# Layer norm of the next tile and the V projection moved into the heads of the K projection

## What is computed

```
xn = layernorm(x)
Q, K, V = xn@Wq+bq, xn@Wk+bk, xn@Wv+bv ; Q, K = rope(Q), rope(K)
s  = softmax(causal(Q K^T / 8)) V @ Wo + bo
g  = silu( layernorm(gelu(xn @ ternary(W_fc)^T)) @ ternary(W_proj)^T )
out = x + s * g
```

## Time and profile before

| what | value |
|---|---|
| median of 3 runs | 6779.58 us (6776.34 to 6803.11) |
| profiled execution, its own time | 6805.19 us |
| its span on the slowest core (core 1) | 6803.5 us |
| PE matmul busy, ACT busy, DVE busy | 48%, 37%, 11% of the span |
| mean granted TensorE clock, die 0 and die 1 | 0.785, 0.791 |
| K/V stage, 836 to 2890 us: busy PE, ACT, DVE | 732.9, 441.5, 266.8 us of 2054 |

### The profile page before, as it was taken

The page is one execution under the profiler, slowest core; times in us unless marked ns, Lnnn a source line. Parts: engine busy times, 40 slices in busy tenths (PEclk is TensorE's granted clock), DMA queues, the critical chain, the costliest instruction groups (busy, mean ns, idle before and its releaser), DMA issues.

```text
span 6803.5 us, 50659 instructions; the slowest of 8 cores (6769.1 to 6803.5 us)
## 1 busy us (share of the span) xinstructions
PE 3262.8 (48%) x13195; PEld 1049.8 (15%) x13195; DVE 766.9 (11%) x1887; ACT 2532.9 (37%) x4503; POOL 355.5 (5%) x598
## 2 busy tenths in 40 slices
PE   2333323432343234423566666666666433664666
PEld 0011111111111111111111111111111111121222
DVE  0122111111111111112100000000000121110000
ACT  2211222211221122223567778888888311111000
POOL 0122100000000000000111110100000000000000
PEclk9999966766677667766778888889998655787888
DMA  6311243345334533342111111111110111113222
GB/s 167 102 54 56 41 62 42 42 41 62 42 43 42 58 44 43 39 68 62 40 52 43 43 62 41 52 64 46 35 54 27 40 43 44 41 37 91 62 62 65
DMA packets 280346, 366.16 MB, mean 54 GB/s; under 512 B 149954, under 2 KB 231954, under 8 KB 272914
## 3 DMA queue, kind: packets, MB, share of 16 engines
q1 hardware_dynamic: 257922, 285.91, 22.0%
q10 hardware_dynamic: 4608, 43.26, 2.1%
q0 software_dynamic: 17552, 33.78, 2.0%
HBM read 299.50 MB, written 71.83 MB: 55 GB/s over the span
## 4 chain that ended last, share of the span: by engine, by line
PE 28%; ACT 28%; DMA 15%; issue 11%; DVE 8%; SPq 6%; POOL 2%; ACTq 1%; DVEq 0%; POOLq 0%
ACT Pbuf L689 11%; ACT Pbuf L692 8%; PE pb L414 5%; PE pb L838 5%; PE pb L485 4%; PE pb L940 4%; DMA xtile<-x_kv 3%; DMA wp_dram<-wps 3%; SPq L506 3%; SPq L524 2%; DMA hcol<-h_dram 2%; DMA wf<-Wfc 2%; ACT xnb L395 1%; DVE x2s L375 1%; PE pb L400 1%
## 5 line engine op out<-in xcount | busy, mean ns | idle before, releaser
L689 ACT ACTIVATE Pbuf<-pb,bias 128x512 bf16<-128x512 f32 x896 | 615.7, 687 | 232.6 <-PE pb L668 193.3
L400 PE MATMUL pb<-identb,xnb 128*128 128x128 bf16 x640 | 93.2, 265 | 1268.3 <-ACT xnb L395 1268.3
L710 PE MATMUL pb<-Pbuf,Vbuf 128*65 128x512 bf16 x1152 | 445.1, 386 | 389.7 <-ACT Pbuf L692 387.1
L692 ACT ACTIVATE Pbuf<-pb,bias 128x512 bf16<-128x512 f32 x896 | 609.8, 681 | 0.0
L668 PE MATMUL pb<-Q_sb,Kbuf 64*128 64x512 bf16 x1152 | 464.8, 403 | 0.0
L665 PE MATMUL pb<-Q_sb,Kbuf 64*128 64x512 bf16 x1152 | 464.6, 403 | 0.0
L713 PE MATMUL pb<-Pbuf,Vbuf 128*65 128x512 bf16 x1152 | 445.1, 386 | 0.0
L838 PE MATMUL pb<-xn5t,wfcT 128*128 128x512 bf16 x1024 | 328.5, 479 | 81.2 <-ACT wfcT L830 60.8
L940 PE MATMUL pb<-wpp,hcol 128*128 128x512 bf16 x1024 | 261.7, 420 | 211.1 <-DMA hcol<-h_dram 162.3
L372 ACT ACTIVATE x2s<-xtile 128x1024 bf16<-128x1024 f32 x80 | 84.7, 1058 | 721.0 <-DMA xtile<-x_kv 632.0
L485 PE MATMUL pb<-Wv_sb,xnT 128*128 128x512 bf16 (+1 forms) x1536 | 306.0, 361 | 76.2 <-ACT vraw L499 76.2
(11 more groups left out here) (170 smaller groups left out, 3990.3 us busy)
## 6 DMA issues: line engine op xcount, KB each, us to landing
xtile<-x_kv SPq DMA_DIRECT2D x64, 512.0 KB, 7.0
V_dram<-vraw SPq DMA_DIRECT2D x128, 132.0 KB, 21.1
Vbuf<-V_dram ACTq DMA_DIRECT2D x8, 2112.0 KB, 14.8
gtile<-Wfc SPq DMA_DIRECT2D x32, 512.0 KB, 3.4
gtile<-Wpj SPq DMA_DIRECT2D x32, 512.0 KB, 3.9
pj_f<-Wpj SPq DMA_DIRECT2D x8, 2048.0 KB, 8.0
t1s<-T1k SPq DMA_DIRECT2D x16, 1024.0 KB, 22.2
t2s<-T2k SPq DMA_DIRECT2D x16, 1024.0 KB, 22.9
```

Of the source, the lines that this page charges most:

```text
L400: pv = E("tensor", lambda e, fc=fc: e.transpose(tr_ps[:, fc * 128:(fc + 1) * 128], xnb[:, fc * 128:(fc + 1) * 128], identb[:]), waits=[("a ...
L689: e1 = E("scalar", lambda e, it=it, blo=blo: e.activation(out=Pbuf[it][:, 0:QTW], in_=sA[it][:, 0:QTW], func=AF.Exp, scale=0.125, bias=blo ...
L692: e2 = E("scalar", lambda e, it=it, bhi=bhi: e.activation(out=Pbuf[it][:, QTW:2 * QTW], in_=sB[it][:, 0:QTW], func=AF.Exp, scale=0.125, bi ...
L710: p1_ = E("tensor", lambda e, vsrc=vsrc, vcb=vcb, it=it, kc=kc, ntile=ntile: e.matmul(cA[0:65, 0:QTW], vsrc[:, vcb:vcb + 65], Pbuf[it][:, ...
```

## The change

The x loads, layer norm and transposes of tile 0 now stand ahead of the loop. For the others, `ln_and_transpose` is a generator that yields ahead of each of its four bodies, and `v_build` is split into `v_build_sub` (one sub of 128 rows) and `v_build_out` (the stores). A `filler` is called once a head within `rope_project`, between the projection of the next head and `keo` of this one: in odd heads it emits one sub of V of this tile, and in each head it advances the generator for the next tile by one step. The copy to `xnT` also waits for the PE work emitted before this tile. The tables are issued ahead of the heads of their tile, as before. The Q stage keeps its order.

```diff
-    def ln_and_transpose(x_src, tt, xnT_buf, marks, tw):
+    def ln_and_transpose(x_src, tt, xnT_buf, marks, tw, key):
         for sub in range(tw // 128):
+            yield
             i = sub % 2
...
-                in_=tr_ps[:].rearrange("p (f t) -> p f t", f=8)), waits=[("pe", pv)], inc="ac")
+                in_=tr_ps[:].rearrange("p (f t) -> p f t", f=8)),
+                waits=[("pe", pv), ("pe", marks.get(key + "_pefree", 0))], inc="ac")
             marks["tr_evac"] = av4
-        return av4
+            marks[key] = av4
...
         pmark = {0: emit_proj(0)}
+        filler = marks.pop("filler", None)
         for hp in range(HP):
             ei = hp % 2
             if hp + 1 < HP:
                 pmark[hp + 1] = emit_proj(hp + 1)
+            if filler is not None:
+                filler(hp)
...
-    def v_build(xnT_buf, tt, tw, marks):
+    def v_build_sub(xnT_buf, tt, tw, marks, subs):
         i = 0
         segs = [(0, 512), (512, 1024), (1024, VROW)]
-        for sub in range(tw // 128):
+        for sub in subs:
...
+    def v_build_out(tt, tw, marks):
+        i = 0
         av = M("ac")
...
+    gen = ln_and_transpose(x_kv, 0, xnT[0], marks, 512, "lnk0")
+    for _ in gen:
+        pass
     for tt in range(NT1):
         i = tt % 2
...
-        ln_and_transpose(x_kv, tt, xnT[i], marks, 512)
...
+        ni = (tt + 1) % 2
+        emit_tables(tt, T1k, T2k, 512)
         _rope_tab_gate[0] = marks["tab_q"]
-        rope_project(xnT[i][:], Wk_sb, bkc, t1s[i][:], t2s[i][:], ('K', tt), tt, 512, marks)
+        if tt + 1 < NT1:
+            marks[f"lnk{tt+1}_pefree"] = M("pe")
+            nxt = ln_and_transpose(x_kv, tt + 1, xnT[ni], marks, 512, f"lnk{tt+1}")
+        else:
+            nxt = iter(())
+
+        def filler(hp, tt=tt, nxt=nxt):
+            if hp % 2 == 1:
+                v_build_sub(xnT[tt % 2][:], tt, 512, marks, [(hp - 1) // 2])
+            next(nxt, None)
+
+        marks["filler"] = filler
+        rope_project(xnT[i][:], Wk_sb, bkc, t1s[0][:], t2s[0][:], ('K', tt), tt, 512, marks)
         marks["tab_reuse"] = M("dv")
-        v_build(xnT[i][:], tt, 512, marks)
...
+        for _ in nxt:
+            pass
+        v_build_out(tt, 512, marks)
```

More of the change, by code:

```diff
@@ L517, in build, with emit_tables @@
              "vps_reuse": M("ac"), "x2_reuse": M("dv"), "u_dv": M("dv")}
+    def emit_tables(tt, src1, src2, tw):
+        q1 = E("sync", lambda e, tt=tt, src1=src1, tw=tw: e.dma_start(
+            out=t1s[0][:].rearrange("p (h t) -> p h t", h=HP)[:, :, 0:tw],
+            in_=src1[:, :, tt * tw:(tt + 1) * tw].rearrange("h p t -> p h t")),
+            waits=[("dv", marks.get("tab_reuse", 0))], inc="q_t0", incval=16)
+        E("sync", lambda e, tt=tt, src2=src2, tw=tw: e.dma_start(
+            out=t2s[0][:].rearrange("p (h t) -> p h t", h=HP)[:, :, 0:tw],
+            in_=src2[:, :, tt * tw:(tt + 1) * tw].rearrange("h p t -> p h t")),
+            inc="q_t0", incval=16)
+        marks["tab_q"] = ("q_t0", M("q_t0"))
@@ L528, in build @@
-        marks["tab_q"] = ("q_t0", M("q_t0"))
-        ln_and_transpose(x_kv, tt, xnT[i], marks, 512)
-        marks.setdefault("xnT_hold", {})[i] = M("ac")
-        marks["tab_wait"] = marks["tab_q"]
-        _rope_tab_gate[0] = marks["tab_q"]
-        rope_project(xnT[i][:], Wk_sb, bkc, t1s[i][:], t2s[i][:], ('K', tt), tt, 512, marks)
+        ni = (tt + 1) % 2
+        emit_tables(tt, T1k, T2k, 512)
+        _rope_tab_gate[0] = marks["tab_q"]
+        if tt + 1 < NT1:
[3 more added lines that the diff above has]
+            nxt = iter(())
@@ L534, in build @@
+        def filler(hp, tt=tt, nxt=nxt):
[4 more added lines that the diff above has]
+        rope_project(xnT[i][:], Wk_sb, bkc, t1s[0][:], t2s[0][:], ('K', tt), tt, 512, marks)
         marks["tab_reuse"] = M("dv")
-        v_build(xnT[i][:], tt, 512, marks)
-        marks["tr_evac"] = max(marks.get("tr_evac", 0), 0)
-        marks[f"xnT_pe{i}"] = M("pe")
+        for _ in nxt:
+            pass
@@ L538, in build @@
+        v_build_out(tt, 512, marks)
     p1_done_q = M("qs")
     p1_done_pe = M("pe")
-    NQT = OWN // 512 if OWN >= 512 else 1
     QW = min(512, OWN)
@@ L544, in build @@
         i = tt % 2
[L545 to L553, removed]
+        emit_tables(tt, T1q, T2q, QW)
         _rope_tab_gate[0] = marks["tab_q"]
-        ln_and_transpose(x_own, tt, xnT[i], marks, QW)
+        marks[f"lnq{tt}_pefree"] = M("pe")
+        for _ in ln_and_transpose(x_own, tt, xnT[i], marks, QW, f"lnq{tt}"):
+            pass
         av = M("ac")
         for fc in range(8):
-            E("sync", lambda e, fc=fc, tt=tt, i=i: e.dma_start(
+            E("sync", lambda e, fc=fc, tt=tt, i=i, QW=QW: e.dma_start(
                 out=xn_dram[fc, :, tt * QW:(tt + 1) * QW],
                 in_=xnT[i][:, fc * QW:(fc + 1) * QW]), waits=[("ac", av)], inc="q_xn", incval=16)
-        rope_project(xnT[i][:], Wq_sb, bqc, t1s[i][:], t2s[i][:], ('Q', tt), tt, QW, marks)
+        rope_project(xnT[i][:], Wq_sb, bqc, t1s[0][:], t2s[0][:], ('Q', tt), tt, QW, marks)
         marks["tab_reuse"] = M("dv")
-        marks[f"xnT_q{i}"] = M("qs")
     p1b_done = M("ac")
```

## The result

| | before | after |
|---|---|---|
| median | 6801.43 us (10 runs) | 6872.6 us (9 runs) |
| ratio | | 1.0114, 95% interval 1.0086 to 1.0142 |
| same pair on a second chip | 6717.19 us | 6809.0 us, 1.0143, interval 1.0114 to 1.0172 |

The change makes the kernel slower, by 1.1 to 1.4%. The forecast was slower by 2.7%, with a range from 6820 to 7060 us. The sign held, and the norm was moved and not hidden, as forecast; the size was about twice too large, and most of that lies in one term, the wait for the tables. (Against 6779.58 us, the median at hand when it was made, the measured 6872.6 lies 93 us higher.)

What follows compares the result with a forecast made beforehand. No single engine owns the chain; a K/V tile is serial pieces, 136.9 us. With norm moved and table wait exposed, the period becomes 148.6; +182 us on the 6779.6 median gives 6961 us, range 6820 to 7060.

Steps and rivals of the forecast that it cites:

- The norm is moved, not hidden: K/V heads 1 to 4: norm bodies overlap neither V nor the same head's chain; 7.97 us each, four times a tile.
- Rival 1: K/V stage: ACT and DVE do the norm while PE does V and projections; -296 us, 6484 us; chance 0.07.
- The x loads: ACT waits 4.3 us for xtile in heads 2 and 4; projection and V hide the load in 1 and 3.
- The clock: PE in the K/V heads: after near idleness a projection takes 3.4 us, a sub of V the mean, 7.1.
- Rival 2: K/V stage: denser PE work keeps the clock high, so no change; about +1 us, 6781 us; chance 0.10 with nearby cases.
- The tables come about 39.8 us after V_dram: Head 0's first m1 waits for t1s and t2s, taken from the former x wait; 39.2 to 43.4 us.
- The sum: K/V stage: tile 0 +45.0, 14 periods of 148.6 against 136.9 us +163.8, last tile -26.8; together +182 us.
- Rival 3: K/V stage: tables later and V slow throughout; period over 154 us, +270 to +300, 7050 to 7080 us; chance 0.08.

Runs made afterwards that it cites:

- e2: The changed kernel, with the norm's first half ahead of the V casts in ACT's list in heads 1 and 3; ratio to before 0.9896.
- e3: The changed kernel, with the next tile's first two x loads right behind the tables, loads 3 and 4 behind the norm freeing their buffer; ratio to before 1.0057.
- c_after: The changed kernel, unaltered, run again on the second chip beside the kernel before; ratio 1.0143, 6809.0 us.
- e4: The changed kernel, with vraw laid out by head so V stores move runs of 1056 bytes, not 264; ratio to before 0.9702.
- c_before: The kernel before the change, unaltered, profiled again on the second chip; median 6717.19 us.

## Why the forecast was right in sign and wrong in size

**The norm is moved, not hidden: right.** Head 1 took 22.0 us in the mean (22.7 forecast), head 2 15.8 (15.35). e2 shows that the list order is the reason. Rival 1 did not occur.

**The x loads: right.** 120.5/28 = 4.3 us in heads 2 and 4, none in 1 and 3.

**The clock: right for the projections, too dear for V, and by luck right in the sum.** 0.63 in the heads with norm, and projections of 3.60 us (3.4 forecast). But V took 5.7 to 6.5 us from the projection's end to the casts' end in the tile shown, where I took 7.1, and head 6, which I priced at the steady 4.05, took 6.0, since its projection ran slow as well. Head 5 took 13.7 (14.7 forecast) and head 7 9.8 (11.3). The errors have opposite signs: heads 1 to 7 come to 105.0 us against 106.2. Rival 2 did not occur, since the projections stayed slow.

**"The tables come about 39.8 us after V_dram": the step that failed.** I took this distance from the x wait of before, as if the transfer of V and tables took the same time in the new order. It did not: on the same chip it fell from 36.3 to 31.4 us (40.9 to 36.1 in the first pair of profiles, a fall of the same size). It was 35.9 again when e3 moved two x loads forward, but the tile of e3 without them behind its tables has 35.4, so what the distance hangs on is open.

**The sum, on one chip.** In means over the cores: tile 0 +41 us (106.1 to 146.9; forecast +45), 14 periods of +6.2, +87 (forecast +164), the last tile -34 (134.5 to 100.1; forecast -27), together +93 against +182; the spans of the two differ by 91. Of the 89 us missing, 15 times 4.9 = 74 are the tables. The rest is 4 us in tile 0, some 3 in the last tile, whose heads 1, 3 and 5, with V and without norm, took 11.7 to 13.9 us where I had 14.7, and 0.6 us in each of 14 periods.

**Rival 3** (tables later, V slow) went the wrong way: the tables came sooner, and V was quicker. The measured 6872.6 us lies inside 6820 to 7060, but that says little, since the range reached down to a change of 40 us; 22 of the 93 us above 6779.58 are the kernel before, whose ten runs had a median of 6801 us. The change itself was +71 us by the medians and +77 by the ratio (1.14% of 6801 us) in the first comparison and +96 (1.43% of 6717 us) in the second, against +182. The mean period, 144.2 us in the first profile, lies in the 141 to 154 of the forecast, and the 139.4 of the second chip does not.

Left open: why V stores and tables take 4.9 us less in the new order. The runs show the size; x loads behind the tables in their own queue do not explain it tile by tile.

## What to carry to other kernels

Interleaving in program order hid nothing here, because the moved work stood between a wait and the instruction that releases the next step. Look in each engine's list for what stands behind the moved piece, and split it so that its first half stands ahead of the wait. Ask first what a stage's long DMA wait consists of: here a store of 264-byte runs and the loads' place in the queue were worth 9%, and the interleaving as first written cost 1%. When a cover is removed, measure the transfer under it by itself, in the new order if that can be had, since its length need not stay what it was under the cover.

## What the runs showed of the hardware

- Eight V stores of 132 KB each and 2 MB of tables took 31.4 us with runs of 264 bytes on the stores' SBUF side (c_after) and 13.7 us with runs of 1056 bytes (e4), the bytes unchanged. The V stores alone landed after 25.0 and 5.6 us.
- In c_before and e3, x loads issued behind the tables in the same queue began to move before the tables had landed: 216 and 220 packets of 2 KB or more on core 1, against 1 in c_after, which has no such loads.
- The time from the first V store to the landing of the tables moves within one kernel too: 32.1 to 37.9 us from tile to tile in c_before, in the mean of the cores.
- The same kernel's V stores and tables took 40.9 us in one profile and 36.3 in another, and the whole kernel 6801 and 6717 us in the medians. A few per cent on a stage bound by small transfers belong to the chip or the occasion, and a term taken from one profile carries them.
